# Spreading C over the partitions by TensorE transposes behind VectorE's product, in a two-layer kernel on one core

## The chip, the core and the metric

The program runs on one NeuronCore of one Trainium2 chip. TensorE, VectorE, ScalarE and GpSimd compute, SyncE issues most of the DMAs. The metric is the device time of one execution in microseconds (us); less is better.

## What is computed

The reference applies two layers to an image of 256 x 256 positions with 128 channels, each behind a group normalisation and with its input added back. Layer 0 is an attention over rows; it takes the first 3.2 ms of the span and the change doesn't touch it. Layer 1 is a selective scan (Mamba-like) over windows of 8 x 8 positions, in four directions k, with 256 inner channels d and 16 states n:

```
x_dbl = jnp.einsum('bkdl,kcd->bkcl', xs, x_proj_w)
dts, Bs, Cs = jnp.split(x_dbl, [DT_RANK, DT_RANK + D_STATE], axis=2)
dts = softplus(einsum('bkrl,kdr->bkdl', dts, dt_projs_w) + dt_projs_b)
# for each position l of a sequence:
dA = jnp.exp(dt[..., None] * A)
h = h * dA + (dt * u)[..., None] * Bl[:, :, None, :]
y = jnp.einsum('bkdn,bkn->bkd', h, Cl)
```

Bs and Cs are the same for all channels d. The kernel keeps channels on the partitions, so a row of B or C must be spread to all 128 partitions before VectorE or GpSimd can multiply by it.

## The kernel before

Layer 1 works in 128 passes (`NB`), each over four sequences of 128 positions (two windows each): 512 positions by 256 channels, a tile of 128 x 1024 f32. A pass has 4 steps (directions), a step 16 units (states), so 64 units, numbered u = 0 to 63 here. Every unit is this chain:

- ScalarE computes the decay exp(dt*A) into `dA` (even units, PSUM) or `dAs` (odd units), two instructions each (`decay`, L1398).
- The input dt*u*B comes in one of two ways. For even units and unit 7 of a step GpSimd multiplies `dtu` by the row of B that a DMA spread (L1593). The other odd units are "turned": ScalarE scales the transposed `dtuT` by a column of `bT`, four instructions (`scale`, L1420), and TensorE transposes the result into the PSUM tile `dbx`, eight instructions (`fill`, L1225). There is one `dbx`: `fill(v)` waits until scan v-2 is done.
- VectorE scans (L1530) and leaves h in `hst`.
- h is multiplied by C into `hc`. For odd units and unit 10 of a step GpSimd does it, with C spread by DMA (L1607). For the other seven even units VectorE does it (`times_c`, L1538), with C in the PSUM tile `cps`, which TensorE fills (`spread_c`, L1202). There is one `cps`, and the side transposes below use it too.
- TensorE transposes `hc` and adds it to `yps` in PSUM, eight instructions (`total`, L1240).

Every engine runs a list that is written out by hand for the pairs of units u, u+1 (u even), in a loop over the passes. TensorE's list for a pair is: `fill(u+3)`; `total(u-1)`; wait for VectorE's product of u (`s_hc`); side transposes, if there are any; the job of u; `total(u)`; `spread_c(u+2)`; the job of u+1. VectorE's is: scan u+1, product of u (unless GpSimd has it), softplus if due, scan u+2, and so on.

Jobs are the rest of the work, one or none in a slot: the projections of the next step (`xproj` at 0, 16, 32, 49; `dt`, two halves, at 4 and 6, 20 and 22, 36 and 38, 52 and 54), the 3x3 convolution of the next pass, the turning and normalisation of the last one (`unpermute` at 3 and 10, `turn_back` at 19 and 35, `out` at 41). All of them use the one PSUM tile `misc`: TensorE fills it, ScalarE (L1330, L1339 and others) empties it, and TensorE waits for that before the next. For a half of `dt`, ScalarE takes relu (L1339), exp (L1353) and ln (L1355) in turn, between decays, and VectorE closes it with L1513 (`dtv`), right behind its product of the unit two further on.

The side transposes (`SIDE`, at units 4, 10 and 12 of a step) turn `xdbl` and `dtu` of the next step into `cps`; ScalarE copies them out (`bT`, L1408; `dtuT`, L1410).

To spread C in bf16 matmuls without losing f32 precision, the kernel splits B and C into three bf16 parts, `part`: ScalarE casts `misc` (L1332); the two `split` jobs, at the two slots behind `xproj`, subtract what the parts hold already by a matmul with `nident` (L1169), and ScalarE casts the rest (L1336). `spread_c` is one matmul of 96 rows: `selc` picks the row of a state in all three parts and copies it to all partitions.

## Time and profile before

| | us |
|---|---|
| median of 3 runs | 27582.96 |
| lowest and highest | 27577.06, 27606.65 |
| the profiled execution | 27622.95 |
| its span (first to last instruction) | 27621.2 |

| engine | busy in the span | share |
|---|---|---|
| VectorE | 25285.8 us | 92% |
| ScalarE | 23632.0 us | 86% |
| GpSimd | 23358.9 us | 85% |
| TensorE | 21957.3 us | 79% |

The profiled execution took 40 us longer than the median. The first scan of layer 1 starts at 3231.9 us and the last product ends at 27584.6 us, so a pass takes 190.3 us. In this profile a duration is that of one instruction, and neighbours on an engine overlap by 0.1 us or so; what a row of instructions costs its engine is the difference of two starts. "Idle before" names what ended a wait. In the waits, "DVE hc <- PE cps" reads: VectorE stood before an instruction that writes `hc`, until TensorE had written `cps`. PEclk is TensorE's granted clock: 1.00 is 2.4 GHz, 0.50 is 1.2 GHz.

### The profile page before, as it was taken

The page shows a single profiled execution, that of the slowest core. Times are in us where ns is not written, and L with a number is a line of the kernel's source. Part 1 is how long each engine was busy: PE and PEld are TensorE (multiplying, and loading weights), DVE is VectorE, ACT ScalarE, POOL GpSimd, SP SyncE. Part 2 cuts the span into 40 slices and gives each one's busy share as a digit, 9 for nine tenths or more (in the row PEclk, how much of TensorE's full clock was granted, in tenths as well). Part 3 has the DMA queues.
Part 4 walks back from the last instruction along what each step waited for, and adds up shares of the span by engine and source line. Part 5 has one row for each costly group of instructions (what it writes and reads, how often), then busy time and mean ns, then how long its engine had stood idle before and what let it go on. Part 6 is the DMA issues. An engine that isn't in the chain of part 4 may idle for free.

```text
span 27621.2 us, 494663 instructions
## 1 busy us (share of the span) xinstructions
PE 21957.3 (79%) x145198; PEld 16882.3 (61%) x145198; DVE 25285.8 (92%) x23743; ACT 23632.0 (86%) x48522; POOL 23358.9 (85%) x10372
## 2 busy tenths in 40 slices
PE   5888588788887888887888888888788888888887
PEld 1666366666666666666666666666666666666666
DVE  7777599999999999999999999999999999999998
ACT  2677488988989988889898898888898998888988
POOL 4000399999999999999999999999999999999999
PEclk6999799999999999999999999999999999999999
DMA  4111433333333333333333333333333333333333
GB/s 148 48 46 46 150 105 106 107 105 107 106 107 107 107 106 107 106 107 105 107 106 106 106 108 105 108 104 108 105 107 105 108 104 108 106 106 107 106 107 97
DMA packets 2189148, 2868.62 MB, mean 104 GB/s; under 512 B 695002, under 2 KB 964858, under 8 KB 2177786
## 3 DMA queue, kind: packets, MB, share of 16 engines
q1 hardware_dynamic: 2181978, 2803.33, 33.0%
q8 instruction: 1280, 20.97, 0.3%
q10 hardware_dynamic: 4608, 33.82, 0.3%
q14 instruction: 1282, 10.50, 0.1%
HBM read 2667.01 MB, written 169.74 MB: 103 GB/s over the span
## 4 chain that ended last, share of the span: by engine, by line
ACT 28%; PE 25%; issue 18%; DVE 12%; POOL 4%; ACTq 1%; DVEq 1%; DMA 0%; SPq 0%; POOLq 0%
DVE hst L1530 11%; PE yps L1240 7%; ACT dbT L1420 6%; ACT dA L1398 6%; ACT dAs L1398 6%; PE dbx L1225 5%; PE misc L1140 5%; POOL hc L1607 2%; POOL dbu L1593 2%; DVE hc L1538 2%; ACT vab L1353 1%; PE misc L1159 1%; PE misc L1176 1%; PE cps L1216 1%; ACT vab L1339 1%
## 5 line engine op out<-in xcount | busy, mean ns | idle before, releaser
L1593 POOL TENSOR_TENSOR dbu<-dtu,bb 128x1024 f32<-128x1024 f32 x4096 | 9697.6, 2374 | 1209.2 <-DVE hst L1530 1208.3
L1530 DVE TENSOR_TENSOR_SCAN hst<-dA,dbu 128x1024 f32<-128x1024 f32 x4096 | 9336.8, 2279 | 778.1 <-ACT dA L1398 755.9
L1607 POOL TENSOR_TENSOR hc<-hst,cc 128x1024 f32<-128x1024 f32 x4096 | 9743.1, 2379 | 5.6 <-DVE hst L1530 3.7
L1240 PE MATMUL yps<-ident,hc 128*128 128x128 f32 x65536 | 8944.2, 283 | 328.6 <-POOL hc L1607 325.1
L1240 PEld LDWEIGHTS yps<-ident,hc 128*128 128x128 f32 x65536 | 7982.1, 147 | 1824.7 <-issue 1273.4
L1530 DVE TENSOR_TENSOR_SCAN hst<-dAs,dbx 128x1024 f32<-128x1024 f32 x3584 | 8104.2, 2261 | 63.5 <-issue 61.2
L1225 PE MATMUL dbx<-ident,dbT 128*128 128x128 f32 x28672 | 4153.0, 292 | 3329.9 <-DVE hst L1530 2975.1
L1225 PEld LDWEIGHTS dbx<-ident,dbT 128*128 128x128 f32 x28672 | 3391.2, 148 | 4750.2 <-DVE hst L1530 3639.0
L1420 ACT ACTIVATE dbT<-dtuT,bT 128x256 f32<-128x256 f32 x14336 | 6125.1, 495 | 18.2
L1398 ACT ACTIVATE dA<-dtv,aneg 128x508 f32<-128x508 f32 x8192 | 5291.6, 678 | 400.0 <-DVE hst L1530 396.1
L1398 ACT ACTIVATE dAs<-dtv,aneg 128x508 f32<-128x508 f32 x7168 | 4743.7, 710 | 531.0 <-DVE hst L1530 528.8
L1538 DVE TENSOR_TENSOR hc<-hst,cps 128x1024 f32<-128x1024 f32 x3584 | 4298.6, 1199 | 521.9 <-PE cps L1202 312.0
L1619 POOL TENSOR_TENSOR dtu<-dtv,xs 128x1024 f32<-128x1024 f32 x512 | 1210.5, 2364 | 2544.0 <-DVE dtv L1513 2544.0
L1140 PE MATMUL misc<-xg,wconv 128*128 128x512 f32 x4608 | 2275.0, 598 | 10.6 <-DMA xg<-xgp 6.0
L1202 PE MATMUL cps<-part,selc 96*128 96x512 bf16 x3584 | 1375.0, 384 | 143.9 <-ACT dtuT L1410 143.9
L524 ACT ACTIVATE ss<-ss,nmx 128x256 f32<-128x256 f32 x2048 | 1012.4, 497 | 294.5 <-DVE nmx L573 294.5
L1164 PE MATMUL misc<-xdbl,wdt 104*128 104x512 f32 x2048 | 1206.6, 673 | 39.4 <-DVE dtv L1513 37.0
L1593 POOL TENSOR_TENSOR dbu<-dtu,bx 128x1024 f32<-128x1024 f32 x512 | 1218.2, 2379 | 0.0
L1607 POOL TENSOR_TENSOR hc<-hst,bx 128x1024 f32<-128x1024 f32 x512 | 1213.3, 2370 | 0.8 <-DVE hst L1530 0.8
L1530 DVE TENSOR_TENSOR_SCAN hst<-dbx,dbu 128x1024 f32<-128x1024 f32 x512 | 1158.3, 2262 | 0.0
L1140 PEld LDWEIGHTS misc<-xg,wconv 128*128 128x128 f32 x4608 | 809.2, 192 | 378.8 <-issue 320.4
L1410 ACT COPY dtuT<-cps 128x512 f32<-128x512 f32 x1024 | 590.7, 577 | 509.1 <-PE cps L1216 507.7
(187 smaller groups left out, 25145.4 us busy)
## 6 DMA issues: line engine op xcount, KB each, us to landing
bb<-l_bscr SPq DMA_DIRECT2D x1024, 1024.0 KB, 5.7
cc<-l_bscr SPq DMA_DIRECT2D x1024, 1024.0 KB, 5.5
bx<-l_bscr SPq DMA_DIRECT2D x1024, 256.0 KB, 6.1
xg<-xgp SPq DMA_DIRECT2D x512, 85.0 KB, 2.5
xgp<-xb ACTq DMA_DIRECT2D x32, 1032.0 KB, 9.4
xt<-in_x_dram SPq DMA_DIRECT2D x128, 256.0 KB, 2.7
l_xnT<-xo SPq DMA_DIRECT2D x128, 256.0 KB, 2.0
xn<-l_xnT SPq DMA_DIRECT2D x256, 128.0 KB, 2.1
```

The source lines that it names most:

```text
L1140: mm = pe.matmul(misc[:, :], wconv[:, f, t], xg[:, :, dy:dy + 8, dx:dx + 32], start=(t == 0), stop=(t == 8))
L1164: pe.matmul(misc[:, :], wdt[:, KS[step], f], xdbl[0:104, step % 2], start=True, stop=True).then_inc(s_mf, 1)
L1202: pe.matmul(cps[:, :], selc[:, u % NST], part[:, u // NST % 2], start=True, stop=True).then_inc(s_cb, 1)
L1225: mm = pe.transpose(dbx[:, f, p * P:(p + 1) * P], dbT[:, turned_of(v) % 2, p, f * P:(f + 1) * P], ident[:])
L1240: mm = pe.matmul(yps[:, p, f * P:(f + 1) * P], hc[:, u % HB, f * 512 + p * P:f * 512 + (p + 1) * P], ident[:], is_transpose=True, start=fi ...
L1398: last = nc.scalar.activation(out[:, f, :, lo:hi], dtv[:, step % 2, f].rearrange("p (s l) -> p s l", l=P)[:, :, lo:hi], ACT.Exp, scale=ane ...
L1420: last = nc.scalar.mul(dbT[:, turned_of(v) % 2, p], dtuT[:, step % 2, p], bT[:, step % 2, p, st:st + 1])
L1530: nc.vector.tensor_tensor_scan(hst[:, v % 4, way], decays.rearrange("p f c -> p (f c)")[:, way], inputs.rearrange("p f c -> p (f c)")[:, way],
L1538: nc.vector.tensor_tensor(hc[:, v % HB].rearrange("p (f c) -> p f c", f=2), hst[:, v % 4].rearrange("p (f c) -> p f c", f=2), cps[:].unsqu ...
L1593: nc.gpsimd.tensor_tensor(to, dtu[:, step % 2], row.unsqueeze(1).to_broadcast([P, 2, 512]), ALU.mult).then_inc(s_inp, 1)
L1607: nc.gpsimd.tensor_tensor(hc[:, v % HB].rearrange("p (f c) -> p f c", f=2), hst[:, v % 4].rearrange("p (f c) -> p f c", f=2), row.unsqueez ...
L1619: nc.gpsimd.tensor_tensor(dtu[:, step % 2], dtv[:, step % 2], xs[:, KS[step] % 2], ALU.mult).then_inc(s_dtu, 1)
```

## The change

C is no longer spread by a bf16 matmul. The side transposes of `xdbl` put B and C, with positions on the partitions, into `cps` already; ScalarE now copies both (`bcT`, 32 columns a block for 16). `spread_c` is four PE transposes of f32: each takes one column of `bcT`, repeated 128 times, as the stationary operand, so that all 128 output partitions get the same 128 values of C. With that go `part`, `selc`, `nident`, the cast behind the copy of `xdbl`, and the two `split` jobs of each step, on TensorE and ScalarE. `xproj` gives 40 rows for 104.

TensorE's list is reordered. The wait for VectorE's product of u stands now right behind `fill(u+3)`; behind it come the side transposes, or, in pairs without them, `spread_c(u+2)`; then `total(u-1)`, the job, `total(u)`. In the pairs with side transposes the spread stays behind `total(u)`, since `cps` is taken. Of the 28 spreads of a pass 16 move and 12 stay. Which engine has which product or input (`PLAIN_ODD`, `C_EVEN`) is as it was.

```diff
@@ -937,8 +930,6 @@
         for q in range(4):
             kind = "pre" if q == 3 else "own"
             JOBS[XPROJ[q]] = (kind, "xproj", (q + 1) % 4)
-            JOBS[XPROJ[q] + 1] = (kind, "split", (q + 1) % 4, 1)
-            JOBS[XPROJ[q] + 2] = (kind, "split", (q + 1) % 4, 2)
             JOBS[DT0[q]] = (kind, "dt", (q + 1) % 4, 0)
             JOBS[DT1[q]] = (kind, "dt", (q + 1) % 4, 1)
         for q, u in enumerate((3, 10)):
@@ -1194,12 +1181,13 @@
                             mm = pe.matmul(dst, x1w[:, p * P:(p + 1) * P], ident[:], start=False, stop=True)
                         mm.then_inc(s_mf, 1)
 
-                def spread_c(ph, u):
+                def spread_c(u):
 
                     step = u // NST
-                    if u % NST == 0:
-                        pe.wait_ge(s_me, ph.misc(("own" if step else "pre", "split", step, 2)))
-                    pe.matmul(cps[:, :], selc[:, u % NST], part[:, u // NST % 2], start=True, stop=True).then_inc(s_cb, 1)
+                    for p in range(4):
+                        mm = pe.transpose(cps[:, p * P:(p + 1) * P],
+                                          bcT[:, step % 2, p, u % NST:u % NST + 1].to_broadcast([P, P]), ident[:])
+                    mm.then_inc(s_cb, 1)
 
                 def side(step, k, b):
 
@@ -1274,23 +1262,28 @@
                             fill(u + 3, b)
                         elif u + 3 > UN and not last:
                             fill(u + 3 - UN, b + 1)
+                        c = SIDE.get(u)
+
+                        def spread_next():
+                            if u + 2 < UN and not c_pool(u + 2):
+                                spread_c(u + 2)
+                            elif u + 2 == UN and not last:
+                                spread_c(0)
+                        if not c_pool(u):
+                            pe.wait_ge(s_hc, b * NCD + (c_dve_of(u) + 1))
+                        if ph.has(c):
+                            side(c[1], c[2], at(ph, c[0]))
+                        else:
+                            spread_next()
                         if u:
                             total(u - 1, b)
                         elif not (isinstance(b, int) and b == 0):
                             total(UN - 1, b - 1)
-                        if not c_pool(u):
-                            pe.wait_ge(s_hc, b * NCD + (c_dve_of(u) + 1))
-                        c = SIDE.get(u)
-                        if ph.has(c):
-                            side(c[1], c[2], at(ph, c[0]))
                         job_of(ph, u)
                         total(u, b)
                         if ph.has(c):
                             pe.wait_ge(s_ce, (at(ph, c[0]) * 4 + c[1]) * 3 + (c[2] + 1))
-                        if u + 2 < UN and not c_pool(u + 2):
-                            spread_c(ph, u + 2)
-                        elif u + 2 == UN and not last:
-                            spread_c(ph, 0)
+                            spread_next()
                         job_of(ph, u + 1)
                 n = phases(pe, body)
                 total(UN - 1, NB - 1)
@@ -1327,13 +1320,7 @@
                     elif what == "xproj":
                         n = b * 4 + j[2]
                         wait(act, s_bst, n * 16 - 16)
-                        nc.scalar.copy(xdbl[0:104, j[2] % 2], misc[0:104, :])
-                        wait(act, s_cb, n * (NCD // 4) - NCD // 4)
-                        nc.scalar.copy(part[:, j[2] % 2], misc[0:96, :]).then_inc(s_me, 1)
-                    elif what == "split":
-
-                        r = 64 if j[3] == 1 else 32
-                        nc.scalar.copy(part[0:r, j[2] % 2], misc[0:r, :]).then_inc(s_me, 1)
+                        nc.scalar.copy(xdbl[0:DTR + 8, j[2] % 2], misc[0:DTR + 8, :]).then_inc(s_me, 1)
                     elif what == "dt":
                         step, f = j[2], j[3]
                         nc.scalar.activation(vab[:, f], misc[:], ACT.Relu, bias=dtc[:, KS[step], f:f + 1], scale=-1.0).then_inc(s_soft, 1)
@@ -1405,7 +1392,7 @@
                     n = b * 4 + step
                     act.wait_ge(s_cf, n * 3 + (k + 1))
                     if k == 0:
-                        nc.scalar.copy(bT[:, step % 2], cps[:].rearrange("p (w n) -> p w n", w=4)[:, :, NST:2 * NST]).then_inc(s_ce, 1)
+                        nc.scalar.copy(bcT[:, step % 2], cps[:].rearrange("p (w n) -> p w n", w=4)[:, :, 0:DTR]).then_inc(s_ce, 1)
                     else:
                         nc.scalar.copy(dtuT[:, step % 2, 2 * k - 2:2 * k], cps[:].rearrange("p (w c) -> p w c", w=2)).then_inc(s_ce, 1)
 
```

The rest of the diff drops the tensors, shrinks `wx` and `wdt` from 104 rows or columns to 40, and drops the load of `selc`.

TensorE's order in a pass, first at the pair of units 16 and 17 (names: `dbx` is fill, `yps` total, `misc<-xs,wx` xproj, `cps` the spread). Before:

```order
L1225 MATMUL dbx<-ident,dbT 128x128 [waits s_scan]
L1225 MATMUL dbx<-ident,dbT 128x128 x7
...
L1240 MATMUL yps<-ident,hc 128x128 [waits s_hcp]
L1240 MATMUL yps<-ident,hc 128x128 x7
...
L1159 MATMUL misc<-xs,wx 104x512 [waits s_me]
L1159 MATMUL misc<-xs,wx 104x512
L1240 MATMUL yps<-ident,hc 128x128 [waits s_hc]
...
L1202 MATMUL cps<-part,selc 128x512
...
L1169 MATMUL misc<-part,nident 96x512 [waits s_me]
```

and with the change:

```order
L1213 MATMUL dbx<-ident,dbT 128x128 [waits s_scan]
L1213 MATMUL dbx<-ident,dbT 128x128 x7
L1188 MATMUL cps<-ident,bcT 128x128 [waits s_hc]
L1188 MATMUL cps<-ident,bcT 128x128 x3
...
L1228 MATMUL yps<-ident,hc 128x128 [waits s_hcp]
L1228 MATMUL yps<-ident,hc 128x128 x7
...
L1150 MATMUL misc<-xs,wx 40x512 [waits s_me]
L1150 MATMUL misc<-xs,wx 40x512
L1228 MATMUL yps<-ident,hc 128x128 [waits s_hc]
```

The spread went from behind `total(16)` to behind `fill(19)`, ahead of `total(15)` and xproj, and is four instructions; the split is gone.

Second, from unit 18's end to unit 20's pair, where the side transposes (`cps<-ident,xdbl`) and the first half of `dt` (`misc<-xdbl,wdt`) stand. Before:

```order
L1240 MATMUL yps<-ident,hc 128x128 [waits s_hc]
...
L1202 MATMUL cps<-part,selc 128x512
...
L1185 MATMUL misc<-ident,xcT 128x128 [waits s_ln,s_me]
...
L1240 MATMUL yps<-ident,hc 128x128 [waits s_hcp]
L1240 MATMUL yps<-ident,hc 128x128 x7
L1209 MATMUL cps<-ident,xdbl 128x128 [waits s_hc]
L1209 MATMUL cps<-ident,xdbl 128x128 x3
...
L1164 MATMUL misc<-xdbl,wdt 128x512 [waits s_me]
L1240 MATMUL yps<-ident,hc 128x128 [waits s_hc]
...
L1202 MATMUL cps<-part,selc 128x512 [waits s_ce]
```

and with the change:

```order
L1228 MATMUL yps<-ident,hc 128x128 [waits s_hc]
...
L1172 MATMUL misc<-ident,xcT 128x128 [waits s_ln,s_me]
...
L1197 MATMUL cps<-ident,xdbl 128x128 [waits s_hc]
L1197 MATMUL cps<-ident,xdbl 128x128 x3
...
L1228 MATMUL yps<-ident,hc 128x128 [waits s_hcp]
L1228 MATMUL yps<-ident,hc 128x128 x7
...
L1155 MATMUL misc<-xdbl,wdt 128x512 [waits s_me]
L1228 MATMUL yps<-ident,hc 128x128 [waits s_hc]
...
L1188 MATMUL cps<-ident,bcT 128x128 [waits s_ce]
L1188 MATMUL cps<-ident,bcT 128x128 x3
```

`total(19)`, the row that waits for `s_hcp`, stood ahead of the wait for `s_hc` and of the side transposes; now it stands behind both, between them and `dt`. The same holds for the pairs of units 4, 36 and 52.

## Rows read from the trace of the kernel before

**Rows 1.** The page's head: span of the profiled execution.

```profile
span 27621.2 us, 494663 instructions
```

**Rows 2.** VectorE's waits in layer 1: who for whom, us, times, longest.

```profile
DVE hst L1530 <- ACT dA L1398: 734.5, 338, 3.4
DVE hc L1538 <- PE cps L1202: 303.3, 249, 2.5
DVE hc L1538 <- DVE hst L1530: 105.1, 212, 1.0
...
DVE dtv L1513 <- ACT vab L1355: 38.0, 102, 0.7
```

**Rows 3.** GpSimd's longest wait in the same stretch.

```profile
POOL dbu L1593 <- DVE hst L1530: 1176.8, 1236, 2.1
```

**Rows 4.** TensorE's timeline, units 10 to 12: start, length, engine, line, tiles, count.

```profile
12788.54 0.38 PE L1202 MATMUL cps<-part,selc 96*128 96x512 bf16 x1
12788.76 1.88 PE L1140 MATMUL misc<-xg,wconv 128*128 128x512 f32 x4
...
12792.23 0.60 PE L1216 MATMUL cps<-ident,dtu 128*128 128x128 f32 x4
12792.66 1.88 PE L1140 MATMUL misc<-xg,wconv 128*128 128x512 f32 x4
```

**Rows 5.** VectorE's timeline in the same pass: waits at units 12, 20, 44.

```profile
12789.02 1.22 DVE L1538 TENSOR_TENSOR hc<-hst,cps 128x1024 f32<-128x1024 f32 x1 [1.65 <-PE cps L1202]
...
12810.82 2.29 DVE L1530 TENSOR_TENSOR_SCAN hst<-dA,dbu 128x1024 f32<-128x1024 f32 x1 [2.10 <-ACT dA L1398]
...
12881.51 2.29 DVE L1530 TENSOR_TENSOR_SCAN hst<-dA,dbu 128x1024 f32<-128x1024 f32 x1 [3.17 <-ACT dA L1398]
```

**Rows 6.** ScalarE's timeline, units 16 to 20.

```profile
12806.37 0.59 ACT L1330 COPY xdbl<-misc 104x512 f32<-104x512 f32 x1
12806.86 0.58 ACT L1332 CAST part<-misc 96x512 bf16<-96x512 f32 x1
```

**Rows 7.** TensorE's timeline, units 16 to 18.

```profile
12804.37 1.88 PE L1159 MATMUL misc<-xs,wx 128*104 128x512 f32 x4
```

**Rows 8.** TensorE's timeline at unit 36.

```profile
12858.23 0.60 PE L1185 MATMUL misc<-ident,xcT 128*128 128x128 f32 x4
...
12861.71 0.66 PE L1209 MATMUL cps<-ident,xdbl 128*128 128x128 f32 x4 [0.43 <-DVE hc L1538]
12862.21 1.02 PE L1164 MATMUL misc<-xdbl,wdt 104*128 104x512 f32 x2
12863.07 1.04 PE L1240 MATMUL yps<-ident,hc 128*128 128x128 f32 x8
```

**Rows 9.** ScalarE's timeline at unit 36.

```profile
12863.61 0.68 ACT L1339 ACTIVATE vab<-misc,dtc 128x512 f32<-128x512 f32 x1
...
12866.06 0.63 ACT L1355 ACTIVATE vab<-vab 128x512 f32<-128x512 f32 x1
```

**Rows 10.** VectorE's timeline at units 36 and 38.

```profile
12860.47 1.19 DVE L1538 TENSOR_TENSOR hc<-hst,cps 128x1024 f32<-128x1024 f32 x1
...
12867.07 0.74 DVE L1513 SCALAR_TENSOR_TENSOR dtv<-misc,dtb,vab 128x512 f32<-128x512 f32 x1
```

**Rows 11.** TensorE's timeline where its clock is low, at unit 20.

```profile
12816.45 0.81 PE L1209 MATMUL cps<-ident,xdbl 128*128 128x128 f32 x4 [2.08 <-DVE hc L1538]
12817.06 1.92 PE L1164 MATMUL misc<-xdbl,wdt 104*128 104x512 f32 x2
12818.76 1.76 PE L1240 MATMUL yps<-ident,hc 128*128 128x128 f32 x8
```

**Rows 12.** Busy time in windows: A:B, us, per engine (count), granted clock, DMA.

```profile
12817.10:12820.00 2.90, 2.90 (x9) 1.76 (x9) 2.90 (x2) 2.33 (x7) 2.10 (x2) 0.50 0.00 0
```

**Rows 13.** VectorE's timeline at unit 2.

```profile
12758.48 1.22 DVE L1538 TENSOR_TENSOR hc<-hst,cps 128x1024 f32<-128x1024 f32 x1 [1.21 <-PE cps L1202]
```

**Rows 14.** ScalarE's timeline at unit 4.

```profile
12758.29 1.30 ACT L1398 ACTIVATE dA<-dtv,aneg 128x508 f32<-128x508 f32 x2
```

More of the change, by code:

```diff
@@ L665, in layer1 @@
     UN = 4 * NST
+    DTR = 2 * NST
     HB = 4
@@ L709, in layer1 @@
         pbwd = sb("pbwd", [P, 2, P])
-        selc = sb("selc", [96, NST, P], BF16)
         wconv = sb("wconv", [P, 2, 9, P])
         wz = sb("wz", [P, 2, P])
-        wx = sb("wx", [P, 4, 2, 104])
-        wdt = sb("wdt", [104, 4, 2, P])
+        wx = sb("wx", [P, 4, 2, DTR + 8])
+        wdt = sb("wdt", [DTR + 8, 4, 2, P])
         wo = sb("wo", [P, 2, P])
@@ L733, in layer1 @@
         xdbl = sb("xdbl", [P, 2, 512])
-        part = sb("part", [96, 2, 512], BF16)
         vab = sb("vab", [P, 2, 512])
@@ L743, in layer1 @@
         dtuT = sb("dtuT", [P, 2, 4, 256])
-        bT = sb("bT", [P, 2, 4, NST])
+        bcT = sb("bcT", [P, 2, 4, DTR])
         dbT = sb("dbT", [P, 2, 4, 256])
@@ L804, in _ @@
                         (pbwd[:], T["pbwd"].rearrange("o l q -> l o q")),
-                        (selF, T["selc"]),
                     ]
@@ L831, in _ @@
                     last.then_inc(s_scaled, 1)
-                    nc.vector.tensor_copy(selc[:], selF)
                     nc.vector.tensor_scalar(dtc[:], dtb[:], -1.0, 20.0, ALU.mult, ALU.add)
@@ L857, in _ @@
                             dve.wait_ge(s_tp, n + 1)
[L858 to L861 removed]
+                            nc.vector.tensor_copy(wx[:, k, f, 0:NST], misc[:, 8 + NST:8 + 2 * NST])
+                            nc.vector.tensor_copy(wx[:, k, f, NST:DTR], misc[:, 8:8 + NST])
+                            nc.vector.tensor_copy(wx[:, k, f, DTR:DTR + 8], misc[:, 0:8]).then_inc(s_cp, 1)
                             n += 1
@@ L1158, in job @@
                         for f in range(2):
-                            mm = pe.matmul(misc[0:104, :], wx[:, KS[step], f], xs[:, KS[step] % 2, f],
+                            mm = pe.matmul(misc[0:DTR + 8, :], wx[:, KS[step], f], xs[:, KS[step] % 2, f],
                                            start=(f == 0), stop=(f == 1))
@@ L1163, in job @@
                         step, f = j[2], j[3]
-                        pe.matmul(misc[:, :], wdt[:, KS[step], f], xdbl[0:104, step % 2], start=True, stop=True).then_inc(s_mf, 1)
+                        pe.matmul(misc[:, :], wdt[:, KS[step], f], xdbl[0:DTR + 8, step % 2], start=True, stop=True).then_inc(s_mf, 1)
                     elif what == "gate":
                         pe.matmul(misc[:, :], wz[:, j[2]], xg[:, :, 1:9, 1:33], start=True, stop=True).then_inc(s_mf, 1)
-                    elif what == "split":
-                        pe.matmul(misc[0:96, :], nident[:], part[:, j[2] % 2], start=False, stop=True,
-                                  skip_group_check=True).then_inc(s_mf, 1)
                     elif what == "unpermute":
@@ L1419, in scale @@
                     for p in blocks:
-                        last = nc.scalar.mul(dbT[:, turned_of(v) % 2, p], dtuT[:, step % 2, p], bT[:, step % 2, p, st:st + 1])
+                        last = nc.scalar.mul(dbT[:, turned_of(v) % 2, p], dtuT[:, step % 2, p], bcT[:, step % 2, p, NST + st:NST + st + 1])
                     if blocks[-1] == 3:
@@ L1680, in shape_constants @@
     pbwd = np.stack([np.ascontiguousarray(pfwd[:, o * P:(o + 1) * P].T) for o in range(2)])
-    selc = np.zeros((96, 16, P), np.float32)
-    for part in range(3):
-        for n in range(16):
-            selc[32 * part + n, n, :] = 1.0
     group = np.kron(np.eye(P // 4), np.full((4, 4), 0.25)).astype(np.float32)
-    return {"group": group, "ident": np.eye(P, dtype=np.float32), "pfwd": pfwd, "pbwd": pbwd, "selc": selc}
+    return {"group": group, "ident": np.eye(P, dtype=np.float32), "pfwd": pfwd, "pbwd": pbwd}
 def build(nc, given, out, N):
@@ L1693, in build @@
     second = {name[len("L1_conv_"):]: ap for name, ap in given.items() if name.startswith("L1_conv_")}
-    consts = {name: given[name] for name in ("ident", "group", "pfwd", "pbwd", "selc")}
+    consts = {name: given[name] for name in ("ident", "group", "pfwd", "pbwd")}
     layer0(nc, {**first, **consts, "l0_ln_w": first["ln_w"], "l0_ln_b": first["ln_b"], "x": given["x"], "x1T": x1T, "xgp": xgp}, N)
```

24 lines of the change are left out of this document (8 added, 16 removed).

## The prediction, made before the run

> **What bounds the kernel now.** The profiled execution spans 27621.2 us [rows 1]. I read the waits of VectorE first, then those of GpSimd, and then followed one pass (the one that starts at 12746.8 us) on the timelines. VectorE is the fullest engine, and its waits in layer 1 are few in kind: 734.5 us for ScalarE's decay `dA`, 303.3 us for TensorE's `cps`, 105.1 us named after its own scan, 38.0 us for ln in front of `dtv` [rows 2]. Divided by 128 passes: 5.7, 2.4, 0.8 and 0.3 us of a pass of 190.3 us. GpSimd waits mainly for VectorE's scans, 1176.8 us [rows 3], so it follows with about 9 us of slack a pass. Hence a microsecond more on VectorE's chain costs a microsecond, and at most some 5% can be won before GpSimd is the bound.
>
> The waits sit at fixed units: 1.65 us before product 12, 2.10 us before scan 20, 3.17 us before scan 44 [rows 5], 1.21 us before product 2 [rows 13]. Which engine is late differs. From unit 10 to unit 20 TensorE works without a pause: its rows there follow each other start to end [rows 4], and product 12 waits for its spread. Before scan 20 ScalarE is late, with the copies behind xproj and four normalisations ahead of the decay. Before scan 44 it is late from unit 36 on: relu at 12863.61 starts an unbroken chain with the table loads of silu at its end.
>
> **The change, part by part.**
>
> ScalarE loses the cast of `part` and two casts in the split slots per step, each about 0.58 us long [rows 6], so some 2.2 us a step gross. Where ScalarE was ahead of VectorE this is worth nothing, and the split slots (1, 2, 17, 18, 33, 34, 50, 51) lie behind or far from the late places: scan 20 waits for a decay that comes ahead of the split of slot 17, scan 44 for work from unit 36 on. Only the cast right behind xproj stands in a late chain, ahead of scan 20; the rows start 0.49 us apart, so -0.49 there.
>
> TensorE: a spread costs 0.22 us from start to next start; four transposes cost 0.43 us (the side transposes, the same shape) [rows 4]. So +0.21 a spread. The stationary operand is a repeated column, which no row shows; its cost is bounded by the same four transposes with plain operands (0.43 us) below and by their slowest row, 0.81 us [rows 11], above. I take 0.43: 128 columns are loaded either way. The spread also ends later: 0.60 us long for 0.38. Each split matmul gone gives back some 0.2 us.
>
> Units 10 to 20. Product 12 waits for a spread that stays in its place behind the side transposes: +0.21. Up to xproj at 16 there are three spreads on TensorE (for 12, 14, 16), +0.63, and the fourth (for 18) now stands ahead of xproj, +0.43. Xproj, which ended at 12806.25, ends 1.06 us later [rows 7]; ScalarE had taken it at 12806.37, nearly at once [rows 6]. So decay 20 comes 1.06 - 0.49 = 0.57 us later. The wait before scan 20 takes up the other shifts of the stretch: **+0.55 us** a pass.
>
> Units 4, 20, 36, 52, the main term. In these pairs there is no `fill` (unit 7 is not turned), so TensorE idles until VectorE's product of u is done. Before, it used that gap for `total(u-1)`; now total stands behind the product and ahead of `dt`. At unit 36: the product ends at 12861.66 [rows 10]; call this T. Side transposes start at T+0.05, `dt` ends at T+1.57 [rows 8]; relu starts at T+1.95, held by ScalarE itself; ln ends 3.08 us after relu's start [rows 9]; `dtv` starts at T+5.41, which is when VectorE is free [rows 10]. So VectorE stands still as soon as `dt` ends later than about T+2.25. With total in front (1.04 us long, 0.88 from start to start, since neighbours overlap by 0.16 as `dt` and total do [rows 8]), `dt` ends at T+2.45: +0.2 us before `dtv`, and at unit 36 ScalarE's whole chain to scan 44 moves by 0.54 us.
>
> That holds at 2.4 GHz. TensorE's granted clock falls to 1.2 GHz behind an idle stretch: at unit 20, after 2.08 us of idling, side transposes, `dt` and total take 0.81, 1.92 and 1.76 us for 0.66, 1.02 and 1.04 [rows 8, 11], with the granted clock at 0.50 [rows 12]. The change lengthens just these idle stretches, since total and the splits no longer break them up. At unit 36 it is from the end of turn_back, 12858.83, to 12861.71, 2.9 us [rows 8]. By the same count (fill 0.9, spread 0.43, two totals 1.75, the job, then nothing until the product) it is about 4.4 us at unit 20, 2.9 at unit 52, and 1.6 at unit 4, where unpermute fills it. At half speed throughout, `dt` ends at T + 0.05 + 0.87 + 1.76 + 1.92 = T+4.6, and `dtv` comes at T+7.76, 2.35 us late. A low stretch may begin or end within the work; I take `dt` at T+3.9, `dtv` 1.65 us late (and 1.9 at unit 20, with the longest idling). Chances of the low clock by the idle lengths: unit 20 surely, 52 0.9, 36 0.8, 4 0.5. That gives, net of the 0.1 to 0.3 us which these places wait already: unit 4 **+0.9**, unit 20 **+1.9**, unit 36 **+1.6** (ScalarE 2.0 us later when low, felt at scan 44), unit 52 **+1.4**.
>
> Small terms: products 28 and 60 wait for a spread that stays behind `total`, +0.15 and +0.22. Product 2 no longer waits for its spread, 1.21 us [rows 13] in about two passes of three (there are 249 waits for `cps` in 128 passes [rows 2], the others mostly at product 12), but decay 4 starts at 12758.29, lasts 1.30 and so ends when the delayed product 2 is nearly done [rows 13, 14]: with product 2 earlier, scan 4 waits for the decay, and xproj ahead of it is 0.45 us later while the cast gone gives 0.49. So -0.1. The wait before product 16 goes into the wait before scan 20: 0. The load and cast of `selc` at the start go: I put -5 us once, an estimate that no row carries and that weighs nothing. SyncE's and GpSimd's lists don't change.
>
> **Sum.** 0.55 + 0.9 + 1.9 + 1.6 + 1.4 + 0.37 - 0.1 = 6.6 us a pass; times 128 is 845 us, less 5 is 840. The profiled execution took 27622.95 us, so 28463; it stands 40 us above the median, so the forecast for the median is **28420 us**, 3.0% slower. GpSimd, which follows VectorE, hides nothing of it.
>
> The Trainium skill (TensorE: Matmul & The Clock Gate, Part 4: PE-mode transpose) says that transpose mode does not count as busy for the clock gate in the way matmuls do. By that rule the half-speed stretches would spread, since 28 bf16 spreads and 8 split matmuls a pass give way to transposes; the trace speaks against it, as layer 1 is mostly transposes already and a stretch of side transposes, `dt` and total keeps its full speed. What it would make here is rival B.
>
> **Rivals.**
>
> A. The clock stays up in the four places (TensorE's idling is broken by something, or 2.9 us don't suffice). Then 0.55 + 3 x 0.2 + 0.54 + 0.27 = about 1.95 us a pass: 27583 + 250 - 5, about 27830 us. For it: in this pass the side transposes of unit 36 ran at full speed (0.66 us) though of the 2.9 us before them only one total of about 1 us was work [rows 8].
>
> B. The clock is low over the whole of the work at all four places: three times 2.35, 2.7 at unit 36 (relu at T+4.65 for T+1.95), plus 0.55 and 0.27, which is 10.6 us a pass and 28930 us. A repeated column that costs 0.81 us for 0.43 ends near there too: 28 spreads at 0.38 us more, of which a third is felt, put 450 us on the forecast.
>
> C. Faster. The spreads come behind the product at once, ScalarE has some 2 us a step less, and `dt` doesn't reach VectorE: then the waits for `cps` and those named after VectorE's own scan go, 303.3 + 105.1 us, and a part of the 734.5 for `dA`, say 90. That gives 27583 - 500 = 27080 us. It decides at one point, whether `dt` ends ahead of T+2.25; against it stands the sum T+2.45 at full speed, and that the waits at 12, 28 and 60 belong to spreads which the change leaves where they were.
>
> D. Nothing that can be measured: 12 of 28 spreads don't move, and the gains and losses cancel: 27583 +- 50.
>
> **How the numbers follow.** Forecast 0.68 (28000 to 28750), A 0.14, B 0.07, C 0.07, D 0.04. About 0.2% can be told from no change, 55 us. The range from 27800 to 28850 takes in A's upper part and B's lower part and leaves out C and D. Slower 0.88, same 0.05, faster 0.07.
>
> **What would show it.** In the profile after: VectorE's wait for ln before `dtv` grows from 38 us to several hundred (right if 400 to 900); TensorE's granted clock is low in nearly every pass at units 20 to 23 and in most at 36 and 52, with side transposes behind an idle stretch of 2.5 us or more; wait for `dA` up from 734.5 us to 900 or more, at scan 20 about 0.35 and at scan 44 above 3.17 us; product 12 waits 1.9 us; wait for `cps` before product 2 gone and one for `dA` before scan 4 in its place. The forecast is wrong if `dt` still ends by T+2.2, if the low clock doesn't come, or if the four transposes take another time than 0.43 us.

## The result: 2.4% slower, and the profile after

The changed kernel takes 28266.9 us (median of 4 runs, 28216.7 to 28312.5) against 27592.0 us (27577.1 to 27606.7) of the kernel before on the same chip: ratio 1.0244, 95% interval 1.0226 to 1.0263. The forecast was 28420 us, in a range from 27800 to 28850. In the profiled execution (28216.7 us) the mean granted clock is 0.934, for 0.946 before:

```profile
span 28214.8 us, 509634 instructions
...
PE 23350.4 (83%) x154926; PEld 17994.1 (64%) x154926; DVE 25331.2 (90%) x23725; ACT 22977.9 (81%) x46986; POOL 23354.4 (83%) x10372
```

ScalarE is busy 654 us less, TensorE 1393 us more, VectorE 45 us more. The medians differ by 675 us, the two profiled executions by 594, since the one after is the fastest of its four. So the time is to be sought in VectorE's waits. They answer to [rows 2], GpSimd's line to [rows 3] (who for whom, us, times, longest), over about 125 passes before and after:

```profile
DVE hst L1517 <- ACT dA L1385: 787.7, 285, 3.5
DVE hc L1525 <- PE cps L1188: 556.4, 398, 3.3
DVE hc L1525 <- issue: 201.0, 95, 2.1
DVE dtv L1500 <- ACT vab L1342: 178.5, 463, 0.4
...
POOL dbu L1580 <- DVE hst L1517: 1777.0, 1830, 4.9
```

The line that names "issue" shows waits for which the profile has no releaser. Nearly all of them stand before product 12, after as before:

```profile
DVE hc L1538 <- issue: 87.7, 46, 1.9
```

The wait for a spread grew most, from 303.3 to 556.4 us; the one for ln before `dtv` went from 38.0 to 178.5, in 463 places instead of 102; the wait for `dA` only from 734.5 to 787.7. The waits without a releaser went from 87.7 to 201.0 and those named after VectorE's own scan from 105.1 to 6.6, so part of this is one wait under another name, and the table by units is the safer reading. GpSimd merely waits longer for VectorE.

The table is worked out from the timelines: each wait of over 0.15 us as a mean over all 128 passes, and in how many of 126 passes (all but the first and the last) the granted clock was low for a part at least of the unit named.

| where VectorE waits | kernel before, us a pass | after, us a pass | clock low: passes before / after |
|---|---|---|---|
| scan 1 | 0.49 | 0.70 | 87 / 116 at 1 |
| product 2 | 0.80 | 0 | |
| scan 4; `dtv` of unit 4 | 0; 0 | 0.12; 0.30 | 0 / 0 at 4 and 5 |
| scan 12 and product 12 | 2.25 | 2.31 | 80 / 32 at 10 |
| product 16 | 0.26 | 0 | |
| scans 19 and 20 | 2.08 | 2.78 | |
| product 22; `dtv` of unit 20 | 0; 0.09 | 1.45; 0.37 | 89 / 126 at 22 |
| product 28 | 0.28 | 1.05 | 44 / 108 at 25 |
| product 38; `dtv` of unit 36 | 0; 0.04 | 1.31; 0.40 | 14 / 116 at 38 |
| scan 44 | 3.18 | 3.43 | |
| product 54; `dtv` of unit 52 | 0; 0.13 | 0.14; 0.36 | 37 / 9 at 54 |
| product 60; scan 62 | 0.88; 0 | 0.06; 0.37 | 126 / 9 at 60, 0 / 117 at 57 |
| all waits of a pass | 10.77 | 15.29 | |
| the pass | 190.30 | 195.08 | |

The pass grew by 4.78 us, of which 4.51 are waits. The first scan of layer 1 came 15.6 us earlier (3216.3 for 3231.9). In the kernels below that keep `selc` and the splits it starts at 3233.2 and 3234.5, in those without them at 3223.5 to 3229.0, so some 3 to 8 us of this come with what the change takes away.

For some products the wait and the low clock belong together pass by pass. In the kernel before, product 60 waits in all 126 passes, and the clock is low at unit 60 in all of them; product 2 waits in exactly the 84 in which it is low at unit 2. After, product 38 waits in exactly the 116 passes in which the clock is low at unit 38 and product 22 in all 126, while product 60 waits only in the 9 passes in which it is low.

TensorE at unit 20 in the pass that begins at 12955 us (start, length, engine, line, tiles, count, idle before):

```profile
13024.62 1.12 PE L1197 MATMUL cps<-ident,xdbl 128*128 128x128 f32 x4 [5.21 <-DVE hc L1525]
13025.53 1.91 PE L1228 MATMUL yps<-ident,hc 128*128 128x128 f32 x8
13027.37 1.14 PE L1155 MATMUL misc<-xdbl,wdt 40*128 40x512 f32 x2
13028.44 1.10 PE L1228 MATMUL yps<-ident,hc 128*128 128x128 f32 x8
13029.37 0.60 PE L1188 MATMUL cps<-ident,bcT 128*128 128x128 f32 x4
```

It answers to [rows 11]. TensorE idled 5.21 us for 2.08: `total(19)` now stands behind the wait, the splits are gone, and the spread for product 20 comes earlier. The side transposes take 1.12 us and total 1.91; `dt` is in part fast again. The granted clock (before the DMA columns) is 0.50 in this stretch and in the same one of unit 36:

```profile
13024.70:13027.40 2.70, 2.70 (x13) 2.37 (x13) 2.70 (x2) 1.96 (x6) 1.89 (x2) 0.50 0.00 0
13071.90:13074.60 2.70, 2.70 (x12) 2.40 (x12) 2.70 (x2) 2.02 (x6) 2.70 (x3) 0.50 0.02 8
```

The side transposes of units 36 and 52, each behind an idle stretch of nearly the same length, the first slow and the second not:

```profile
13071.88 1.12 PE L1197 MATMUL cps<-ident,xdbl 128*128 128x128 f32 x4 [2.80 <-DVE hc L1525]
...
13121.52 0.66 PE L1197 MATMUL cps<-ident,xdbl 128*128 128x128 f32 x4 [2.67 <-DVE hc L1525]
```

VectorE at units 22 and 38, behind the work of units 20 and 36; the last row answers to [rows 5]:

```profile
13030.01 1.22 DVE L1525 TENSOR_TENSOR hc<-hst,cps 128x1024 f32<-128x1024 f32 x1 [1.07 <-PE cps L1188]
13031.66 0.75 DVE L1500 SCALAR_TENSOR_TENSOR dtv<-misc,dtb,vab 128x512 f32<-128x512 f32 x1 [0.43 <-ACT vab L1342]
...
13077.53 1.22 DVE L1525 TENSOR_TENSOR hc<-hst,cps 128x1024 f32<-128x1024 f32 x1 [1.33 <-PE cps L1188]
13079.18 0.75 DVE L1500 SCALAR_TENSOR_TENSOR dtv<-misc,dtb,vab 128x512 f32<-128x512 f32 x1 [0.43 <-ACT vab L1342]
...
13093.89 2.29 DVE L1517 TENSOR_TENSOR_SCAN hst<-dA,dbu 128x1024 f32<-128x1024 f32 x1 [3.43 <-ACT dA L1385]
```

The reader is to see two waits where the prediction had one. In these pairs the spread for the next product still stands last in TensorE's list: side transposes, `total(u-1)`, `dt`, `total(u)`, spread. What makes `dt` late makes the spread later still, and product u+2 stands ahead of `dtv` on VectorE. So most of the delay shows as a wait for `cps`.

### The profile page after: what moved, and what is told of

It reads as the page before. It is cut to its first block, busy times and chain, and to the rows that moved or that the text cites. A ratio compares the mean times of both kernels' runs of the same rounds, so it can differ in the third digit from the quotient of the medians.

```text
span 28214.8 us, 509634 instructions
## 1 busy us (share of the span) xinstructions
PE 23350.4 (83%) x154926; PEld 17994.1 (64%) x154926; DVE 25331.2 (90%) x23725; ACT 22977.9 (81%) x46986; POOL 23354.4 (83%) x10372
## 4 chain that ended last, share of the span: by engine, by line
PE 27%; issue 21%; DVE 19%; ACT 14%; POOL 6%; DVEq 1%; ACTq 0%; POOLq 0%
DVE hst L1517 14%; PE yps L1228 8%; PE misc L1131 6%; ACT dA L1385 6%; DVE hc L1525 5%; PE dbx L1213 4%; POOL dbu L1580 3%; POOL hc L1594 3%; PE misc L1155 2%; ACT dAs L1385 2%; PE cps L1197 2%; PE cps L1188 1%; ACT dbT L1407 1%; ACT vab L1340 1%; PE cps L1204 1%
## 5 line engine op out<-in xcount | busy, mean ns | idle before, releaser
L1228 PEld LDWEIGHTS yps<-ident,hc 128*128 128x128 f32 x65536 | 8178.4, 152 | 1798.8 <-issue 1626.1
L1228 PE MATMUL yps<-ident,hc 128*128 128x128 f32 x65536 | 9277.3, 293 | 29.5 <-DVE hc L1525 2.9
L1407 ACT ACTIVATE dbT<-dtuT,bcT 128x256 f32<-128x256 f32 x14336 | 6124.3, 495 | 18.7
L1213 PE MATMUL dbx<-ident,dbT 128*128 128x128 f32 x28672 | 3943.7, 282 | 1948.6 <-DVE hst L1517 1824.6
L1188 PE MATMUL cps<-ident,bcT 128*128 128x128 f32 x14336 | 2300.1, 284 | 336.0 <-ACT dtuT L1397 215.2
L1188 PEld LDWEIGHTS cps<-ident,bcT 128*128 128x128 f32 x14336 | 1612.4, 139 | 710.2 <-DVE hc L1525 409.3
L1197 PE MATMUL cps<-ident,xdbl 128*128 128x128 f32 x2048 | 445.7, 356 | 1562.5 <-DVE hc L1525 1562.5
L1197 PEld LDWEIGHTS cps<-ident,xdbl 128*128 128x128 f32 x2048 | 285.2, 176 | 1705.9 <-DVE hc L1525 1704.4
L1326 ACT ACTIVATE vab<-misc,dtc 128x512 f32<-128x512 f32 x1024 | 695.4, 679 | 709.9 <-PE misc L1155 709.9
L1155 PE MATMUL misc<-xdbl,wdt 40*128 40x512 f32 x2048 | 1226.5, 680 | 3.6 <-DVE dtv L1500 2.9
```

The costliest lines, as they stand in the source:

```text
L1155: pe.matmul(misc[:, :], wdt[:, KS[step], f], xdbl[0:DTR + 8, step % 2], start=True, stop=True).then_inc(s_mf, 1)
L1188: mm = pe.transpose(cps[:, p * P:(p + 1) * P], bcT[:, step % 2, p, u % NST:u % NST + 1].to_broadcast([P, P]), ident[:])
L1197: mm = pe.transpose(cps[:, p * P:(p + 1) * P], xdbl[:, step % 2, p * P:(p + 1) * P], ident[:])
L1213: mm = pe.transpose(dbx[:, f, p * P:(p + 1) * P], dbT[:, turned_of(v) % 2, p, f * P:(f + 1) * P], ident[:])
L1228: mm = pe.matmul(yps[:, p, f * P:(f + 1) * P], hc[:, u % HB, f * 512 + p * P:f * 512 + (p + 1) * P], ident[:], is_transpose=True, start=fi ...
L1407: last = nc.scalar.mul(dbT[:, turned_of(v) % 2, p], dtuT[:, step % 2, p], bcT[:, step % 2, p, NST + st:NST + st + 1])
```

## The experiments

Three questions. Which part costs the time, the spread or the order? How much of it comes through TensorE's clock? Can the cost be bought back? Ratios are against the kernel before, run on the same chip.

### The order alone

The kernel before, bf16 spreads, splits and casts kept, with the list of TensorE in the new order: the hunk in `body` of the diff, nothing else.

> The kernel before with TensorE's new order alone: the wait for VectorE's product right behind fill, then side transposes or the bf16 spread, then total(u-1); splits, casts and selc stay. Theory (the order costs, by delaying dt at units 4, 20, 36, 52 and by the idle stretches that lower the clock): most of the loss is here, 28050 to 28300 us, with waits before products 22 and 38 as in the changed kernel. Rival (the f32 transposes of a repeated column cost): within 0.5% of the kernel before, below 27720 us.

Measured: 28238.6 us, 1.0218 (1.0201 to 1.0235). Its waits:

```profile
DVE hst L1535 <- ACT dA L1403: 1028.5, 403, 3.4
DVE hc L1543 <- PE cps L1202: 418.5, 360, 2.2
DVE dtv L1518 <- ACT vab L1360: 149.4, 291, 0.9
```

The order by itself costs about as much as the whole change, but not by the same waits. Those before products 22 and 38 and before `dtv` are there with the bf16 spread, the first two smaller (0.87 and 0.44 us a pass, for 1.45 and 1.31). The largest is another: scan 4 waits 1.83 us a pass, for 0.12 in the changed kernel. It goes with the clock: in the 75 of 126 passes in which xproj of unit 0 ran slowly (over 2.1 us long, for 1.88) it was 2.81 us in the mean, in the others 0.45. In the changed kernel that xproj ran slowly in one pass.

### The spread alone

The changed kernel with the list in the old order:

```diff
+                        if u:
+                            total(u - 1, b)
...
                         if not c_pool(u):
                             pe.wait_ge(s_hc, b * NCD + (c_dve_of(u) + 1))
                         if ph.has(c):
                             side(c[1], c[2], at(ph, c[0]))
-                        else:
-                            spread_next()
-                        if u:
-                            total(u - 1, b)
...
-                            spread_next()
+                        spread_next()
```

> The changed kernel with TensorE's old order: total(u-1) ahead of the wait, every spread behind total(u). It has the transposes and the lighter ScalarE alone. Theory: some 0.2 us more before each of products 2, 12, 16, 28 and 60 and before scan 20, less up to 0.3 us from casts that are gone: 27590 to 27720 us. Rival (the transposes cost): 28000 us or more.

Measured: 27813.1 us, 1.0061 (1.0045 to 1.0078). Four transposes for one matmul, with the splits and casts gone, cost 0.6%, more than expected. Scan 20 gains (1.31 us for 2.08), but product 2 waits 1.35 us for 0.80, product 22 1.33 for nothing and product 60 1.23 for 0.88. So the wait before product 22 comes with either part alone, also with total in its old place; whether the transposes or the missing splits bring it here, no run separates. The two parts add up to 2.8% where both together give 2.4%.

### Total ahead of the product again

The changed kernel with `total(u-1)` back ahead of the wait, in all pairs and in the four pairs of units 4, 20, 36 and 52 alone:

```diff
+                        if u:
+                            total(u - 1, b)
...
                         if not c_pool(u):
                             pe.wait_ge(s_hc, b * NCD + (c_dve_of(u) + 1))
                         if ph.has(c):
                             side(c[1], c[2], at(ph, c[0]))
                         else:
                             spread_next()
-                        if u:
-                            total(u - 1, b)
...
```

> The changed kernel with total(u-1) ahead of the wait for the product in all pairs; the spread still stands right behind the product. Theory: dt ends again near T+1.6 at units 4, 20, 36, 52 and the waits before products 22 and 38 go, while the gains before products 2 and 60 stay: 27450 to 27650 us. Rival (the cost is in the number of transposes or in xproj being later): 28000 us or more.

> The changed kernel with total(u-1) ahead of the wait only in the four pairs of a pass that have no fill (units 4, 20, 36, 52). If these four places are the whole of it, the time is that of the kernel with total first everywhere, within 0.3%: 27450 to 27650 us. If the late xproj (units 0, 16, 32) matters as well, it is slower than that one by 0.4 us a pass or more, 50 us.

Measured: in all pairs 27724.3 us, 1.0033 (1.0021 to 1.0044); in the four alone 27829.2, 1.0071 (1.0054 to 1.0087). So 2.1 of the 2.4 per cent hang on the place of total, 1.7 of them on the four pairs that the main term spoke of. These are net figures. The wait for ln before `dtv` is gone, and so is the one before product 38. But product 22 still waits 1.56 us, with the clock low at unit 22 in all 126 passes, behind 3.31 us of idling. TensorE at unit 20 with total first:

```profile
12853.16 1.12 PE L1197 MATMUL cps<-ident,xdbl 128*128 128x128 f32 x4 [3.32 <-DVE hc L1525]
12854.21 2.07 PE L1155 MATMUL misc<-xdbl,wdt 40*128 40x512 f32 x2
12856.21 1.97 PE L1228 MATMUL yps<-ident,hc 128*128 128x128 f32 x8
12857.98 1.06 PE L1188 MATMUL cps<-ident,bcT 128*128 128x128 f32 x4
```

The list is shorter by one total, yet all of it runs at the low clock, and the spread ends no earlier: 5.9 us behind product 20 in the mean, for 5.8 in the changed kernel. In the kernel before it ended 3.8 us behind, and product 22 never waited, though the clock was low at unit 22 in 89 passes. The four alone are 105 us slower than total first in all pairs; scan 4 waits 0.81 us a pass there and not at all in the other. That both stayed slower than the kernel before was not expected.

### The clock held up by unread work

The changed kernel with matmuls that nobody reads, in the idle stretches ahead of units 20 and 36: 3 and 1 ahead of `turn_back`, and one behind it at each. They write `misc` between two jobs. This is added work; the outputs are as they were.

```diff
+                def fill_idle(ph, job_after, n):
+                    pe.wait_ge(s_me, ph.misc(job_after) - 1)
+                    for _ in range(n):
+                        pe.matmul(misc[:, :], wo[:, 0], xdbl[:, 0], start=True, stop=True)
...
+                        if u in (20, 36):
+                            fill_idle(ph, JOBS[u], 1)
                         if not c_pool(u):
```

> The changed kernel, order as it is, with work added: matmuls whose result nobody reads (wo times xdbl, written to misc and overwritten by the next job) in TensorE's idle stretches ahead of the products of units 20 (three ahead of turn_back, one behind) and 36 (one and one). Theory (the long idle stretch lowers the clock and that makes the larger part of the loss at 20 and 36): side transposes, total, dt run at full speed there, the waits before products 22 (1.45 us a pass) and 38 (1.31) go to nearly 0, the wait before dtv falls to 0.2 to 0.3: 3 us a pass less, 27850 to 28000 us. Rival (the order alone costs, the clock plays no part): no gain from more work, 28200 us or more.

Measured: 27852.4 us, 1.0083 (1.0066 to 1.0100), as expected. TensorE at unit 20, and VectorE behind it:

```profile
12880.08 1.12 PE L1261 MATMUL misc<-xdbl,wo 128*128 128x512 f32 x2 [1.61 <-ACT g L1343]
12881.10 0.66 PE L1198 MATMUL cps<-ident,xdbl 128*128 128x128 f32 x4
12881.60 1.04 PE L1229 MATMUL yps<-ident,hc 128*128 128x128 f32 x8
12882.56 1.12 PE L1156 MATMUL misc<-xdbl,wdt 40*128 40x512 f32 x2
12883.62 1.09 PE L1229 MATMUL yps<-ident,hc 128*128 128x128 f32 x8
12884.55 0.60 PE L1189 MATMUL cps<-ident,bcT 128*128 128x128 f32 x4
```

```profile
12885.35 1.20 DVE L1535 TENSOR_TENSOR hc<-hst,cps 128x1024 f32<-128x1024 f32 x1
12886.84 0.75 DVE L1510 SCALAR_TENSOR_TENSOR dtv<-misc,dtb,vab 128x512 f32<-128x512 f32 x1 [0.30 <-ACT vab L1352]
```

The same list of work now takes 4.05 us instead of 5.35, from the side transposes to the spread's end. The waits before products 22 and 38 are gone, and 0.28 to 0.39 us are left before each of the four `dtv`, which is what `dt` at T+2.64 costs at full speed (T is the end of VectorE's product of u). With more work on TensorE the program is 415 us faster by the times, 445 by the ratios (1.0244 to 1.0083): about two thirds of the loss came through the clock. By the profile the pass is 3.4 us shorter; 2.76 of them are the waits before products 22 and 38, and 0.60 are before product 28, where the clock was low in 108 passes and is now in 14, though nothing was added there.

### Can it be bought back? Three steps

Total first in all pairs, with 4 unread matmuls ahead of unit 20 (A); with the spread behind xproj in pairs 0, 16 and 32 besides (B); with the spreads for 12, 28 and 60 ahead of `total(u)` besides (C):

```diff
+    WARM = {19: 4}
...
-                        else:
+                        elif u not in XPROJ:
                             spread_next()
                         job_of(ph, u)
+                        if u in XPROJ:
+                            spread_next()
...
-                        total(u, b)
+                        early = u in (10, 26, 58)
+                        if not early:
+                            total(u, b)
```

> Total first everywhere, plus four unread matmuls ahead of turn_back at slot 19. With total first a wait of 1.56 us a pass before product 22 was left, with 3.3 us of idling ahead of unit 20's product. Theory: it goes, 200 us less than total first alone (27724): 27500 to 27620 us, about the kernel before. Rival: that wait comes from the length of the transposes and stays, 27700 us or more.

> As total first and warm, with the spread of pairs 0, 16 and 32 behind xproj and ahead of total(u). Theory: xproj ends 0.43 us earlier, scan 20 waits 2.1 us for 2.54, 30 to 60 us less than the warm kernel. Rival: scan 20 is held by ScalarE's own list, no difference (within 20 us).

> As the last, with the spreads for products 12, 28 and 60 behind the job and the side copy but ahead of total(10), total(26), total(58). Theory (product 12 waits for TensorE's list alone): its wait of 1.9 us falls by the total and the two dsd matmuls ahead of it, 1.3 us, product 28's by 0.4: 1.3 to 1.9 us a pass, 27250 to 27400 us, ahead of both kernels. Rival: GpSimd or ScalarE takes the place of the wait (scan 14 or 20 later by as much), within 50 us of the last.

Measured: A 27722.3 us, 1.0036 (1.0022 to 1.0050); B 28044.8, 1.0150 (1.0133 to 1.0167); C 28025.8, 1.0145 (1.0128 to 1.0162). All three missed, and in one way: each did what it was made for, and the gain was lost in another place. In A product 22 no longer waits (1.56 us with total first alone), but total and spread around the seam of two passes run slowly, xproj with them, and VectorE waits 1.48 us more ahead of scan 4. TensorE there:

```profile
12779.94 1.10 PE L1214 MATMUL dbx<-ident,dbT 128*128 128x128 f32 x8 [2.02 <-DVE hst L1525]
12780.88 1.57 PE L1229 MATMUL yps<-ident,hc 128*128 128x128 f32 x8
12782.24 1.06 PE L1189 MATMUL cps<-ident,bcT 128*128 128x128 f32 x4
12783.23 2.59 PE L1151 MATMUL misc<-xs,wx 128*40 128x512 f32 x4
```

In B scan 20 waits 2.11 us for 2.54, as predicted. But the clock was low at units 25 (110 of 126 passes), 38 (94) and 60 (115). Product 60 pays most, 1.91 us a pass for 0.59 in A, then product 38 (0.89 for nothing), scan 29 (0.75) and product 28 (1.00 for 0.42):

```profile
12994.85 2.29 DVE L1527 TENSOR_TENSOR_SCAN hst<-dAs,dbx 128x1024 f32<-128x1024 f32 x1 [1.06 <-PE dbx L1214]
12998.30 1.22 DVE L1535 TENSOR_TENSOR hc<-hst,cps 128x1024 f32<-128x1024 f32 x1 [1.16 <-PE cps L1189]
```

In C product 12 waits 0.70 us for 1.92 in B, but product 14 now waits 0.93, product 2 1.08 and scan 1 1.31. Over 126 passes of layer 1 the low stretches add up to 1905 us with total first alone, 1369 in A, 3273 in B and 2301 in C; in the kernel before they are 2055 us and in the changed one 2816.

### The seam of two passes kept busy

A and C with 3 unread matmuls at the end of pair 56 and 2 at the end of pair 62, and the kernel before with these five alone:

```diff
+    TAIL = {57: 3, 63: 2}
...
+                        if u + 1 in TAIL and not last:
+                            pe.wait_ge(s_me, ph.misc(("pre", "dt", 0, 1)))
+                            for _ in range(TAIL[u + 1]):
+                                pe.matmul(misc[:, :], wo[:, 0], xdbl[:, 1], start=True, stop=True)
```

> Total first everywhere and the four unread matmuls at slot 19, as in f6, plus unread matmuls where that kernel idles ahead of low stretches of the clock: three at the end of pair 56, two at the end of pair 62. In f6 the wait before product 22 went (1.56 us a pass) but one before scan 4 came (1.48), with the low clock moved to units 1 to 3. Theory (the clock's low stretches move about the pass and take the gain back): with units 57 to 3 kept at full speed the waits before scan 4 (1.48) and product 60 (0.59) go, 2 us a pass, 27430 to 27560 us. Rival (scan 4 waits for ScalarE's own list): 27700 us or more.

> As g9, with xproj ahead of the spread in pairs 0, 16, 32 and with the early spreads for products 12, 28, 60 (as f8). In f8 the waits at product 12 and scan 20 fell by 1.65 us a pass but others came with a low clock at units 1, 25, 38, 43 and 59. Theory: with the seam kept warm the waits before product 2 and 60 go (2.0 us a pass in f8), 27250 to 27450 us, ahead of both kernels. Rival: low stretches at units 25 and 38, which nothing here keeps warm, take it back: 27600 us or more.

> The kernel before, nothing else changed, with the same unread matmuls at the ends of pairs 56 and 62. Theory (low stretches cost in that kernel too): the waits before products 2 (0.80 us a pass) and 60 (0.88) shrink to under 0.3 together, about 150 us: 27430 to 27530 us. Rival: those waits are of the spread's place in the list, no change, 27600 to 27660 us.

Measured: A with the seam 27564.8 us, 0.9979 (0.9969 to 0.9988); C with the seam 27746.2, 1.0043 (1.0026 to 1.0060); the kernel before with the seam **27505.7**, 0.9956 (0.9939 to 0.9972), the fastest of all. A's wait before scan 4 fell to 0.18 us a pass, its clock rose to 0.970, and its low stretches fell to 802 us. In C the earlier spreads did cut product 12 to 0.67 us, but products 14, 28 and 38 wait 0.93, 0.16 and 0.64, with the clock low at unit 25 in 124 of 126 passes. The kernel before lost at least 0.4% to the low clock: with the seam busy its waits before products 2 and 60 fall from 0.80 and 0.88 us a pass to 0.04 and 0, and the pass by 0.84, while scans 1, 48 and 62 wait 0.95 more. Its wait for `cps` is

```profile
DVE hc L1551 <- PE cps L1204: 124.7, 82, 1.7
```

for 303.3 us in [rows 2], at the same number of spreads. Its low stretches still add up to 1669 us, twice those of A with the seam, which is slower: what counts is where the clock is low, and whether VectorE comes to wait there.

## Why the prediction was right, point by point

The direction came out, and so did the two parts of the main term: `dt` later by the total in front of it, and a low clock behind longer idling. The size came out partly by luck: the sum was 6.6 us a pass and the pass grew by 4.78, with terms that were 3.1 us too large and others 1.1 too small. Most of the added wait stands before another instruction than the text says, and at unit 20 not for the reason that it gives. Its terms:

- **Four transposes at 0.43 us.** Right: the next instruction starts 0.44 us behind the first of the four in the rows above, and over all 14336 instructions one lasts 284 ns, as those of `fill`, with plain operands, do (282 ns in layer 1):

```profile
L1188 PE MATMUL cps<-ident,bcT 128*128 128x128 f32 x14336 | 2300.1, 284 | 336.0 <-ACT dtuT L1397 215.2
```

- **Units 10 to 20, +0.55.** Measured: scans and product 12 +0.06, product 16 -0.26, scans 19 and 20 +0.70, together +0.50. The product alone waits 2.05 us; 1.9 was expected.
- **Unit 4, +0.9.** Over-sized; +0.30. `dt` ended at T+2.66, 0.2 us past the T+2.45 of full speed, and the clock stayed high, for which the text gave an even chance. The idle stretch was 1.5 us long, as counted.
- **Unit 20, +1.9.** Right in size, +1.7 (product 22 +1.45, `dtv` +0.28), but the place was wrong. I followed `dt` to `dtv` alone, and not the spread that stands at the end of the same list, which product 22 needs sooner. `dt` ended at T+4.12 in the mean (T+3.9 was taken), and the stretch of idling was 5.2 us, not 4.4. That the size fits is luck as well: with total back in front only the 0.28 before `dtv` go and product 22 waits 1.56, and with the old order throughout it waits 1.33. What all of these have in common is a slow stretch at unit 20, not the place of total. Why product 22 waits there is open in this much: either part of the change brings it alone.
- **Unit 36, +1.6.** Measured +1.92: product 38 +1.31, `dtv` +0.36, scan 44 +0.25. Most of what I put on scan 44 is taken up by the wait before product 38. Here the place of total is the cause: with total in front the clock is never low at unit 36, and the waits before product 38 and `dtv` are gone.
- **Unit 52, +1.4.** The term that was most over-sized: +0.37. I gave the low clock a chance of 0.9 from an idling of 2.9 us. It was 2.67 us, and the clock was low (at unit 54) in 9 of 126 passes, fewer than the 37 before; `dt` ended at T+2.71. At unit 36, with 2.80 us, it was low in 116, and in the order alone, with 2.93 us, `dt` ended at T+3.19 and product 38 waited only 0.44. The length of the idling alone doesn't settle it.
- **Product 28, +0.15.** Under-sized: +0.77. The stretch from unit 25 runs at the low clock in 108 of 126 passes, which no step of the sum had.
- **Product 60, +0.22.** Wrong sign: -0.82, and +0.37 before scan 62 behind it. The 0.88 us before were a slow stretch, low in 126 of 126 passes, which is gone from there. The text put the waits for `cps` in the kernel before at products 2 and 12; about a third of the 249 stood before product 60.
- **Product 2, -0.1.** -0.80, and scan 4 takes back only 0.12. The step that failed is that decay 4 would be as late as the product had been. It isn't the casts and splits that are gone: in the kernel before with the seam busy, which keeps them, product 2 waits 0.04 us and scan 4 doesn't wait. Scan 4 waits where xproj of unit 0 runs slowly: 2.81 us against 0.45 in the order alone, 2.49 against 0.71 in A, which has no casts. And the wait before product 2 was itself of the low clock, not of the spread's place.
- **Start, -5 us.** It was -15.6 in this execution; the other kernels without `selc` and the splits came 3 to 8 us earlier than the kernel before.

The overestimates (0.6 at unit 4, 1.0 at 52, 0.6 at product 2, 0.7 at product 60, 0.2 at unit 20) outweigh the under-sized terms (0.32 at 36, 0.62 at product 28, 0.21 at scan 1, which the sum left out). Nearly all of them are judgements of where the clock is low. Rival A, with the clock up, stood at 27830 us, and the kernel with the two stretches kept busy ran at 27852; the nearness is in part chance, since the gains at products 2 and 60 are not in A's sum. Rival B fell with the price of the column and with units 4 and 52; rival C needed `dt` by T+2.25, and it ended at T+2.64 at best. The gross saving of ScalarE is 1.7 us a step (three casts of 0.58), not the 2.2 a step of the text, and its busy time fell by 1.3 a step (654 us over 512 steps): neighbours overlap, and the copy to `bcT` takes 244 ns for 191. No term rested on it. The waits were divided by 128 passes where the window holds about 125.6, which makes `dA` 5.8 us a pass and not 5.7.

Of the signs named ahead: the wait for ln reached 178.5 us and not 400 to 900, since product u+2 took the delay. The wait for `dA` reached 787.7, not 900; scan 20 grew by 0.46 for 0.35, scan 44 is above 3.17. The clock was low at 22 and 38 as said, and not at 52 to 54.

**What stays open.** Why the low stretches lie where they do. In four kernels (A, B, C, C with the seam) a saving at one place came with slow stretches at another, and no rule read from idle lengths places them: 2.67 us of idling and 2.80 us gave opposite results. What the clock costs at a known place is shown by the kernels with unread work. Where it would fall next was foreseen in the recorded text of C with the seam alone, as its rival (units 25 and 38).

## What to carry to other kernels

When work moves behind a wait on an in-order engine, follow everything in its list up to the next wait, and ask which of its results is needed first; here it was the last item, the spread, and not the one that seemed critical. Work in front of a wait also kept TensorE busy. Taken away, it left a low clock at unit 36; at unit 20 the clock was low with total in either place. The low clock was about two thirds of the loss here. Putting the order back didn't bring all of it back, so keep the size of a wait apart from the cause that the forecast named for it, and take away one cause at a time. Before reordering a tuned kernel, try whether a few unread matmuls in its idle stretches pay; five a pass won 0.4% on the kernel before, more than any reordering did, while four at another place won nothing (1.0033 to 1.0036).

## What the runs showed of the hardware

A PE transpose whose stationary operand is one column read 128 times costs what a plain one does, 284 ns long and 0.44 us for four. At the granted clock of 0.50 such a group of four took 1.06 us for 0.60 from first start to last end (total first, unit 20), and eight plain transposes 1.91 for 1.04. In layer 1 of the changed kernel 116,672 of TensorE's 135,004 instructions are transposes, 15.6 of its 21.0 ms of busy time, and the mean granted clock there was 0.942. The Trainium skill (TensorE: Matmul & The Clock Gate, Part 4: PE-mode transpose) says that transpose mode doesn't count as busy for the clock gate as matmuls do. These figures speak against it as far as it would keep the clock low in a layer of transposes; whether a transpose counts for somewhat less than a matmul, no run here shows. Over the whole span the mean granted clock of the kernels lies between 0.926 and 0.970. I had not expected that adding matmuls which nobody reads makes both kernels faster, by 415 us in the changed one (28266.9 to 27852.4) and by 0.44% (0.28 to 0.61) in the kernel before, nor that the low stretches of a program add up to 802 to 3273 us in kernels that differ in the order of a few instructions and in a few unread matmuls.
